# Two pairs of expert tiles in one trip of TensorE to its row halves

## The reference, cut to what matters

```
logits = flat @ router_w;  top 2 of softmax, their weights made to sum to 1
h = silu(einsum('td,edf->etf', flat, w1))      # d = 256, f = 512, e = 8
y = einsum('etf,efd->etd', h, w2)
out = einsum('etd,te->td', y, cw)              # cw is 0 but for the top 2
```

## Time and profile before

| | |
|---|---|
| median of 3 runs | 1869.44 us (1864.21 to 1869.96) |
| profiled execution, span | 1874.5 us, 28,123 instructions |
| TensorE busy | 1720.6 us, 92% |
| VectorE, ScalarE, GpSimd busy | 58%, 49%, 9% |
| the experts' stage | about 128 to 312 us |

### The profile page before, as it was taken

How to read it: one execution, slowest core, us unless ns; L and a number is a source line. 1 busy time by engine, 2 the same in 40 slices (tenths; PEclk the granted TensorE clock), 3 DMA queues, 4 the chain that set the end, 5 groups by cost and what they waited for, 6 DMA issues and landing times.

```text
span 1874.5 us, 28123 instructions
## 1 busy us (share of the span) xinstructions
PE 1720.6 (92%) x8536; PEld 1011.7 (54%) x8537; DVE 1081.5 (58%) x2991; ACT 916.7 (49%) x2195; POOL 171.2 (9%) x281
## 2 busy tenths in 40 slices
PE   5879997779999999999999999999999999999996
PEld 2548885455555555555555555545555555555564
DVE  7763332465665666556656665566565655565652
ACT  2213332456464646454646464546464646464642
POOL 5023342110020002000200020002000000000000
PEclk8759998789999999999999999999999999999999
DMA  7714443110010011000100110001001000000000
GB/s 232 281 40 131 123 122 77 57 35 12 1 35 1 1 34 35 23 13 1 35 1 1 34 35 23 13 1 35 1 1 35 12 23 1 1 1 1 1 23 12
DMA packets 59107, 72.31 MB, mean 39 GB/s; under 512 B 16644, under 2 KB 44888, under 8 KB 58840
## 3 DMA queue, kind: packets, MB, share of 16 engines
q1 hardware_dynamic: 50088, 58.77, 9.6%
q0 software_dynamic: 5376, 10.76, 2.3%
q10 hardware_dynamic: 3504, 1.06, 0.2%
HBM read 50.64 MB, written 19.92 MB: 38 GB/s over the span
## 4 chain that ended last, share of the span: by engine, by line
PE 69%; DVE 7%; issue 5%; ACT 1%; DMA 0%; DVEq 0%; POOL 0%; ACTq 0%; another core or an unknown queue 0%; POOLq 0%
PE pj L1447 17%; PE pj L1535 16%; PE pj L1541 7%; PE pj L1513 6%; PE sc L1470 6%; PE ob L1496 4%; PE pt L1481 4%; PE pj L1455 2%; PE pj L1437 1%; DVE pT L1349 1%; PE pj L1505 1%; DVE swapped L1724 1%; PE pj L1519 1%; PE pj L1547 1%; PE pj L1523 1%
## 5 line engine op out<-in xcount | busy, mean ns | idle before, releaser
L1447 PE MATMUL pj<-wqkv,xT 128*128 128x512 f32 x768 | 347.6, 603 | 5.9 <-issue 5.9
L1535 PE MATMUL pj<-xsq,w 128*128 128x512 f32 (+3 forms) x748 | 318.2, 574 | 6.5 <-DVE hid L1814 4.5
L1616 ACT ACTIVATE prob<-prob,nm 128x256 f32<-128x256 f32 (+1 forms) x512 | 240.5, 471 | 123.1 <-DVE nm L1753 118.3
L1753 DVE CUSTOM_DVE_ANT_0 prob<-sc,mask 128x256 f32<-128x256 f32 (+1 forms) x512 | 170.0, 386 | 132.4 <-issue 132.4
L1447 PEld LDWEIGHTS pj<-wqkv,xT 128*128 128x128 f32 x768 | 145.0, 192 | 183.2 <-issue 181.5
L1535 PEld LDWEIGHTS pj<-xsq,w 128*128 128x128 f32 (+1 forms) x748 | 135.6, 188 | 150.8 <-issue 145.3
L1719 DVE TENSOR_TENSOR direct<-qkraw,tabs 128x1024 f32<-128x1024 f32 x64 | 78.5, 1226 | 132.6 <-ACT qkraw L1587 132.6
L1481 PEld LDWEIGHTS pt<-ident,prob 128*128 128x128 f32 x896 | 105.0, 141 | 91.6 <-issue 65.3
L1481 PE MATMUL pt<-ident,prob 128*128 128x128 f32 x896 | 127.2, 276 | 23.8 <-DVE pT L1349 18.5
L1470 PE MATMUL sc<-kT,qT 64*128 64x256 f32 (+1 forms) x1024 | 132.2, 377 | 14.1 <-DVE nm L1753 14.1
L1541 PE MATMUL pj<-hid,w 128*128 128x512 f32 (+3 forms) x340 | 140.5, 568 | 1.2 <-DVE hid L1814 1.2
(11 more groups left out here) (307 smaller groups left out, 2258.7 us busy)
## 6 DMA issues: line engine op xcount, KB each, us to landing
w1x<-w_folded SPq DMA_DIRECT2D x72, 128.0 KB
slots_y<-yt SPq DMA_DIRECT2D x36, 256.0 KB
x1tok<-in_x_dram SPq DMA_DIRECT2D x10, 512.0 KB, 6.6
w1m<-in_L_ffn_w_dram SPq DMA_DIRECT2D x8, 512.0 KB, 5.7
w2m<-in_L_ffn_w_dram SPq DMA_DIRECT2D x8, 512.0 KB, 8.6
x_after_moe<-x1tok SPq DMA_DIRECT2D x8, 512.0 KB
x1out<-x_after_moe SPq DMA_DIRECT2D x8, 512.0 KB
out_dram<-x1out SPq DMA_DIRECT2D x7, 512.0 KB, 2.9
```

Source lines behind the costliest of these rows:

```text
L1447: mm = pe.matmul(o[:, :], xs(s, c, w * P, P), wqkv[:, l, c, k * INNER:(k + 1) * INNER], start=(c == 0), stop=(c == DC - 1))
L1535: mm = pe.matmul(o[0:P if j == NJ - 1 else HJ[j], 0:tn], cols, h[:, c, t0:t1], start=(c == 0), stop=(c == DC - 1))
L1616: ins = a.activation(prob[:, g % 4, hh, 0:n], prob[:, g % 4, hh, 0:n], ACT.Exp, bias=nm[:, g % 4, hh:hh + 1], scale=-1.0, accum_out=rs[:, ...
L1753: ins = v.tensor_tensor_reduce(prob[:, g % 4, hh, 0:n], sc[par][:, hh, 0:n], mask[:, w % 2, 0:n], -1.0, 3.0e38, ALU.add, ALU.min, nm[:, g ...
```

## The change

TensorE now does the up products of two pairs one after the other, then turn and down for each of two pairs: `up(u+2), up(u+3), turn(u+4), down(u), turn(u+5), down(u+1)`. At the start it turns pairs 0 to 3 and does up for 0 and 1 singly. `hT` has six buffers in place of two; `ub`, `tanh`, `xs` and the result banks stay at two, so `up` waits in addition for the silu of pair `u - 2`. Each half of the result copies has its own semaphore, `y_copied[par]`, and each half of `down` waits for its own bank alone. ScalarE's order over two pairs is new, VectorE's follows TensorE's. The loop body covers the same six pairs.

```diff
-            hT = [sb(f"hT{i}", [P, 2, FC, P]) for i in range(2)]
+            hT = [sb(f"hT{i}", [P, 2, FC, P]) for i in range(NB)]
...
-            y_copied = sem("y_copied")
+            y_copied = [sem(f"y_copied{par}") for par in range(2)]
...
-                        sp.wait_ge(y_copied, u * 2 + 3)
+                        for par in range(2):
+                            sp.wait_ge(y_copied[par], u + 1)
                         sp.dma_start(SY[u], yt[k][:, :, :]).then_inc(y_stored[k], 16)
...
                     def up(u, k, n):
                         pe.wait_ge(w1_in[k % NB], n * 32 + 32)
                         pe.wait_ge(xs_done, u + 1)
+                        wait_done(pe, h_done, u * 2 - 2)
...
                             pe.wait_ge(h_done, u * 2 + (par + 1))
-                            if par == 0:
-                                pe.wait_ge(y_copied, u * 2 + 1)
+                            wait_done(pe, y_copied[par], u)
...
-                    def one(u, k, i, left):
+                    def two(u, k, i, left):
                         if left > 2:
-                            turn_x(u + 2, (k + 2) % NB, i + (k + 2) // NB)
-                        if left > 1:
-                            up(u + 1, k + 1, i + (k + 1) // NB)
-                        down(u, k)
+                            for n in range(2):
+                                up(u + 2 + n, k + 2 + n, i + (k + 2 + n) // NB)
+                        for n in range(2):
+                            if left > 4:
+                                turn_x(u + 4 + n, (k + 4 + n) % NB, i + (k + 4 + n) // NB)
+                            down(u + n, k + n)
...
+                    for n in range(2):
+                        turn_x(n, n, 0)
+                    for n in range(2):
+                        up(n, n, 0)
+                        turn_x(n + 2, n + 2, 0)
+                    pairs_walk(pe, two, 2)
...
                 @block.vector
...
+                    def two(u, k, i, left):
+                        if left > 2:
+                            silu(u + 2, k + 2)
+                            silu(u + 3, k + 3)
+                        for n in range(2):
+                            copy_y(u + n, k + n, i)
...
                 @block.scalar
...
+                    def two(u, k, i, left):
+                        if left > 2:
+                            act(u + 2, k + 2)
+                        if left > 4:
+                            copy_x(u + 4, k + 4)
+                        if left > 2:
+                            act(u + 3, k + 3, (0,))
+                        copy_y(u, k, i)
+                        if left > 2:
+                            act(u + 3, k + 3, (1,))
+                        if left > 4:
+                            copy_x(u + 5, k + 5)
+                        copy_y(u + 1, k + 1, i)
+                    for n in range(2):
+                        copy_x(n, n)
+                    for n in range(2):
+                        act(n, n)
+                        copy_x(n + 2, n + 2)
+                    pairs_walk(a, two, 2)
```

More of the change, by code:

```diff
@@ L1070, in build @@
             tanh = [sb(f"tanh{i}", [P, FC, P]) for i in range(2)]
-            hT = [sb(f"hT{i}", [P, 2, FC, P]) for i in range(2)]
+            hT = [sb(f"hT{i}", [P, 2, FC, P]) for i in range(NB)]
             yt = [sb(f"yt{i}", [P, 2, D]) for i in range(NB)]
-            pace = sb("pace_e", [P, 1])
             xb = ps("xsb", [P, P])
@@ L1091, in wait_done, with pairs_walk @@
                     eng.wait_ge(s, value)
-            def pairs_walk(eng, one):
+            def pairs_walk(eng, one, by=1):
                 with eng.Fori(0, PAIRS // NB - 1) as i:
-                    for k in range(NB):
+                    for k in range(0, NB, by):
                         one(i * NB + k, k, i, PAIRS)
-                for k in range(NB):
+                for k in range(0, NB, by):
                     one(PAIRS - NB + k, k, PAIRS // NB - 1, NB - k)
@@ L1158, in down @@
                             pe.wait_ge(h_done, u * 2 + (par + 1))
-                            if par == 0:
-                                pe.wait_ge(y_copied, u * 2 + 1)
+                            wait_done(pe, y_copied[par], u)
                             for j in range(FC):
-                                mm = pe.matmul(yb[par][:, 0:D], hT[k % 2][:, par, j, :],
+                                mm = pe.matmul(yb[par][:, 0:D], hT[k % NB][:, par, j, :],
                                                w2m[:, bass.ds(e, 1), j, :].rearrange("p o d -> p (o d)"),
@@ L1183, in _ @@
                         v.memset(yt[k][:, :, :], 0.0).then_inc(y_stored[k], 16)
-                    v.memset(pace[:, :], 0.0).then_inc(y_copied, 1)
                     def silu(u, k):
@@ L1188, in silu, with copy_y @@
                             v.wait_ge(tanh_done, u * 2 + (par + 1))
-                            v.scalar_tensor_tensor(hT[k % 2][:, par, :, :], tanh[par][:, :, :], 1.0, ub[k % 2][par][:, :, :],
+                            v.scalar_tensor_tensor(hT[k % NB][:, par, :, :], tanh[par][:, :, :], 1.0, ub[k % 2][par][:, :, :],
                                                    ALU.add, ALU.mult).then_inc(h_done, 1)
-                    def one(u, k, i, left):
-                        if left > 1:
-                            silu(u + 1, k + 1)
+                    def copy_y(u, k, i):
                         v.wait_ge(y_full, u * 2 + 2)
                         v.wait_ge(y_stored[k], i * 16 + 16)
-                        v.tensor_copy(yt[k][:, 1, :], yb[1][:, 0:D]).then_inc(y_copied, 1)
-                    silu(0, 0)
-                    pairs_walk(v, one)
+                        v.tensor_copy(yt[k][:, 1, :], yb[1][:, 0:D]).then_inc(y_copied[1], 1)
+                    def two(u, k, i, left):
[5 more added lines that the diff above has]
+                    for n in range(2):
+                        silu(n, n)
+                    pairs_walk(v, two, 2)
                 @block.scalar
@@ L1207, in copy_x, with act @@
                         a.copy(xs[k % 2][:, :], xb[:, :]).then_inc(xs_done, 1)
-                    def act(u, k):
+                    def act(u, k, pars=(0, 1)):
                         a.wait_ge(u_full, u + 1)
-                        for par in range(2):
+                        for par in pars:
                             wait_done(a, h_done, u * 2 + (par - 1))
@@ L1214, in act, with copy_y @@
                                          ).then_inc(tanh_done, 1)
[L1216 to L1220, removed]
+                    def copy_y(u, k, i):
                         a.wait_ge(y_full, u * 2 + 1)
                         a.wait_ge(y_stored[k], i * 16 + 16)
[L1223 to L1227, removed]
+                        a.copy(yt[k][:, 0, :], yb[0][:, 0:D]).then_inc(y_copied[0], 1)
+                    def two(u, k, i, left):
[13 more added lines that the diff above has]
+                        copy_x(n, n)
+                    for n in range(2):
+                        act(n, n)
+                        copy_x(n + 2, n + 2)
+                    pairs_walk(a, two, 2)
         experts.close()
```

4 lines of the change are left out of this document (removed).

## The result

The changed kernel takes 1861.38 us (median of 7 runs, 1857.86 to 1863.8), the kernel before 1866.58 us (7 runs on the same chip, 1864.21 to 1869.96). The ratio is 0.9967, with a 95% interval from 0.9956 to 0.9979: 5.2 us less, by the interval 3.9 to 8.2. The 1869.44 us from which the forecast was worked out were the median of three runs; over all its timings here the kernel before had medians of 1866.6 to 1867.8.

The account below looks back on a forecast made before the run. TensorE's products, one after the other, were taken to bound the experts' stage, with tiling changes on that path. Terms of 6.6 - 0.5 + 0.7 + 0.4 - 0.1 = 7.1 us took 1869.44 to 1862.3 us, range 1858 to 1871.

Parts of the forecast that it names:

- What bounds the kernel: Experts' stage: it costs TensorE's products one after the other; a trip's tiling changes cost 0.39 us beyond its products.
- 17 changes of tiling at 0.39, 6.6 us: Pairs 2 to 35 in 17 double trips: 17 changes there and back disappear, saving 6.6 us.
- The drawing: One double trip timed from its first row-half product, T: next T at T+9.31, where two trips now take 9.74 us.
- Register load, 0.03 a double trip: Sequencer's expert-number load ahead of down: 0.03 us a double trip, 0.5 us over 16; bounds 0 and 5.4.
- Added waits, nothing: Up's wait for an earlier silu and two half signals: cost nothing; 0.1 us a double trip without cover.
- Waits removed, 0.7 and 0.4: Waits before the last down and before down of pair 2 go: gains 0.7 and 0.4 us, together 0 to 1.1.
- The 0.36 us of pair 2: Down of pair 2 stood 0.36 us at 148.42 for its silu; removing that wait was to gain 0.4 us.
- The start, -0.1: Stage start: reordered turns and ups, idle 1.6 against 1.5 us; 0.1 us charged, bounds 0 and 1.7.
- rival (a): Saving partly eaten: load exposed (3 us), clock rises later (1.7 us) or attention-stage clock pattern; gain 2 to 5 us; 22%.
- ScalarE, cost nothing: ScalarE's order in a double trip: tanh from T+2.7, y copy done by T+5.1, 0.35 us to spare, no cost.
- Rival (b): Late tanh makes ScalarE's order the bound; second down stands 1.3 us, 1883 us; 12% with any other new wait.
- The sum: All terms together: 6.6 - 0.5 + 0.7 + 0.4 - 0.1 = 7.1 us less, median from 1869.44 to 1862.3 us.

Follow-up runs that it names:

- e1: Changed kernel with the first transpose put between the two pairs' up products; 1869.18 us, ratio 1.0004 to the kernel before.
- e3: Changed kernel with ScalarE in plain order, both tanh of the second pair ahead of the x copy and first y copy; 1862.49 us, one execution.
- e9: Changed kernel with ScalarE in plain order, the same kernel as e3, timed over 8 runs; 1862.17 us, ratio 0.9967 to the kernel before.
- e2: Kernel before with the result copies signalled by half and nothing else changed; 1866.09 us, one execution.
- e8: Kernel before, unchanged, run again for a second profile; 1866.11 us.
- e4: Changed kernel with four extra tanh on ScalarE ahead of the first y copy of each double trip; 1870.69 us.
- the warm start: Changed kernel with idle transposes keeping TensorE busy at the stage's start, the kernel of e5, profiled twice; 1866.23 us (12 runs), second profile's execution 1868.08 us.
- e6: Changed kernel with two hT buffers again and VectorE's and ScalarE's orders changed to suit; 1862.70 us.
- e7: Changed kernel with three pairs in one trip, the transpose between the two halves of down; 1860.42 us, ratio 0.9964 to the kernel before.
- e11: Changed kernel, unchanged, run a second time for another profile; 1863.77 us.
- e5: Changed kernel with 56 idle transposes into a spare bank on TensorE at the stage's start; 1866.23 us, ratio 0.9994 to the kernel before.

## Why the prediction was right, step by step

**What bounds the kernel: shown.** e1 changes TensorE's order alone and the gain goes; e3 and e9 change ScalarE's alone and nothing happens. The trace has the 17 groups of 32 row-half products, no wait before the last down, and the last down product ends at 304.33, where some 305 was forecast.

**17 changes of tiling at 0.39, 6.6 us: shown, slightly small.** The double trip was forecast at 9.31 against 9.74 now, and is 9.279 against 9.717: 0.44 less. Over the 15 steady steps that is 6.56 us. The two other changes lie at the start and the end, in the sums below. The drawing and the sum of the prediction don't agree: the drawing saves 9.74 - 9.31 = 0.43 a double trip, the sum takes 0.39 less 0.03 for the load. The runs side with the drawing, in whose double trip the first down product behind a turn is not charged the 0.10 us of the earlier trace rows: the second down product follows after 0.23 us on the mean, before after 0.32.

**Register load, 0.03 a double trip: about right.** The drawing had its chain from T+1.02 to T+2.11; it starts at T+0.92 (196.42) and down's first weight load stands at T+1.99, with the turn's product. Turn to down is 0.16 there and 0.11 at the second turn, so 0.05 a double trip may be the sequencer's, and it is inside the 9.279. The chain lies where a lead of a little over 31 puts it. By the Trainium skill (TensorE: Matmul & The Clock Gate, "Architectural detail: the array is 16× 32×32, not 1× 128×128"), whose queue of 64 instructions gives this estimate, it would have begun at about T, as the double trip's first product did; the traces disagree. The Trainium skill (DMA: Bandwidth & Descriptors, "Latency and other measured facts") has a floor of some 600 ns for the load itself, and that doesn't hold here, as the shortest takes 0.30. Loads near 0.6 us do come: the second half's in single trips (e2). The load that could have cost something takes 0.30. The prediction's median of 0.31 hid these two sorts.

**Added waits, nothing: right in the double trip, not in the single one.** e2 shows 0.04 us a trip where the second half's load is long. The prediction had 0.1 as the price without cover, and hadn't seen that in a single trip the cover is, by the reading given at e2, already used.

**Waits removed, 0.7 and 0.4.** The last wait is gone, through the half signal (e2). By starts it was 308.19 - 303.76 - 3.46 - 0.10 = 0.87 us, more than the 0.71 of the row, whose end is modelled. With the change of tiling that goes there too, the end of the stage is 1.36 us shorter. The 0.36 us of pair 2 can't be seen by itself: it drowns in the first double step. In e8 it is 0.23 us.

**The start, -0.1: mis-sized, inside its bound of 1.7.** The order came as drawn (turn at 136.56, forecast 136.5; down at 140.96, forecast 141), but the first of these times was met by luck: the turn was to wait for ScalarE's x copy, which ends at 134.36, and waited for a gather; and up of pair 2 starts right behind it, at 136.97, as the silu that it waits for had ended at 135.0. What moved is the clock: up at 143.0 instead of 139.9. That is rival (a)'s clock term. The first double step is 12.11 us against 10.57 in e3, where the clock rises at 139.7: 1.5 us. It offsets the change of tiling there, the 0.4 of pair 2 and the shorter wait at 136: up to the up of pair 4 it is 18.08 us, and before it was 21.46, in which one more down of 3.46 is done, so the start is 0.07 us longer than before. Against e8, which has no wait at 136, it is 0.86 us longer. The lone term comes nearer to its upper bound than to the value taken.

**ScalarE, cost nothing: right, for a wrong number.** Tanh was placed at T+2.7, because it lagged its products by 0.57 in the earlier trace rows; it starts at T+1.31. The 0.57 was one execution's (e8). Rival (b)'s mechanism exists and costs once the copy ends past some T+5.4 (e4), but there was 0.9 us to spare rather than 0.35, and the late tanh that carried its 12% is in neither profile of after and not in e8.

**The sum.** The stage was forecast 7.1 us shorter; it is 7.9 shorter by the first profile of before and 7.1 to 7.2 by e8. In parts: 6.56 steady, 1.36 at the end, 0.07 back at the start, 7.85. By the prediction's own terms these parts were 15 x 0.36 = 5.4 steady, 0.39 + 0.7 = 1.1 at the end and 0.36 + 0.4 - 0.1 = 0.7 gained at the start. So the steady part was 1.2 too small and the start 0.7 too large, and the total is nearer than its terms. The runs' medians differ by 5.2, whose interval of 3.9 to 8.2 holds 7.1. That the forecast of 1862.3 lies 0.9 from 1861.38 owes something to chance: it set out from a median 2.9 us too high, and the gain in the medians is 1.9 smaller.

**What stays open** is that difference. The kernels with the shorter stages have more time behind the stage in some executions (4.7 us between two profiles of one kernel), and for the warm start, whose stage is 8 to 10 us shorter than before, the median is only 1.1 us lower, and the interval of its ratio holds 1. Its two profiles show both late stretches at 1.2 GHz, and so does e6; after's two show none and one, e1, e2, e3 and e9 one each, e4, e7 and the two of before none. These stretches are 3 to 10 us in all and the smaller part. What the time behind the stage follows, over all 13 profiles, is the whole time at 1.2 GHz in it, 27 to 48 us of which lie in the first 100 us: with 38 to 42 us of it (five profiles) it is 1552.7 to 1554.2 us, with 44 to 52 (six) 1555.3 to 1559.7, with 55 (two) 1562.6 and 1564.1. That the differences behind the stage come with the clock is seen so in the profiles, though no run set it there; why one start should bring more of it than another is not settled. An earlier rise of the clock did not show in a median either: e9, with 140.4 in its profile, has 1862.17 against the changed kernel's 1861.38.

## What to carry to other kernels

Count the changes of TensorE's tiling in a loop, and measure one by the starts of single products on either side: here 0.4 us there and back, 8% of a single trip, and putting equal tiles behind one another is worth just that. Look at what the sequencer does at the join: a third pair in the trip gave nothing in the steady step, since the sequencer came late for the products behind. Measure a change of a few us by the stretch it touches, from first to last product, and take a second profile of the kernel before ahead of any argument from one late signal or one wait: the span moved by 10 us between two executions of one kernel, the stage by 0.7.

## What the runs showed that was not expected

- A register load ahead of the second half's down takes 0.56 to 0.66 us in most single trips (before, e2, e8), 0.30 in nearly all double trips of the changed kernel, on the same line and address pattern. In e4 and e6 some half of the second half's loads are longer than 0.32 (15 and 17 of 36), up to 0.59, in e1 15 of the first half's. What decides it was not found.
- The same program had tanh some 0.6 us behind its products in most trips, once 2.3, in one execution, and 0.05 to 0.14 in another.
- The granted clock at the start rose at 143.0 and 142.1 for the changed kernel, at 139.7 and 140.4 for e3 and e9, and at 141.2 and 141.3 for e6 and e4, whose TensorE order is the same. The waits ahead of the turns near 133 and 137 don't settle it: 0.22 and 0.78 us in after, 0.20 and 0.79 in e3, 0.27 and 0.79 in e9, 0.29 and 1.13 in e11. What makes it rise later was not found; 3 us of it are 1.5 us of the stage.
- Stretches of 3.4 and 6.8 us at 1.2 GHz, at the same two places some 480 and 860 us behind the stage, came in some executions and not in others, of the same kernel too (after and e11). In e5's two, TensorE had 6 products each, where a window of 8 us of after at 1158 has 24 at 2.4 GHz.
